# An attention and expert kernel: the order of TensorE's first instructions in the expert stage

## The chip, the cores and the metric

The kernel runs on one core of a Trainium2 chip. The metric is the device time of one execution in microseconds (us), told as the median of several runs. The engines of the core are named PE (TensorE matmul), PEld (TensorE weight load), DVE (VectorE), ACT (ScalarE), POOL (GpSimd) and SP (SyncE, which only issues DMAs here).

## The reference

A layer norm, cross attention with 16 heads over 8 sequences of 512 tokens and width 512, and a residual. Then a second layer norm and a layer of 8 experts, two for each token:

```
logits = flat @ router_weight.T + router_bias          # flat: 4096 tokens x 512
scores = softmax(logits); topk_vals, topk_idx = top_k(scores, 2)
w      = zeros(T, E) with topk_vals at topk_idx
gu     = einsum('th,ehf->tef', flat, gate_up_proj) + gate_up_bias
gate   = minimum(gu[..., :512], 7);  up = clip(gu[..., 512:], -7, 7)
act    = (up + 1) * gate * sigmoid(1.702 * gate)
down   = einsum('tei,eih->teh', act, down_proj) + down_bias
out    = einsum('teh,te->th', down, w);  result = x + out
```

## The kernel before, in words

Three stages follow each other: `attention_stage` (to about 970 us of the span), `routing_stage` (to about 1020 us) and `expert_stage`. Only the last is touched.

The expert stage works on 39 tiles of 256 token places; a tile belongs to one expert. For tile i the steps are these. POOL gathers the rows of the tokens into `xg` (`fetch`, L1540) with two indirect DMAs. PE turns them (`turn_rows`, L1279: 8 transposes of 128x128 into two PSUM tiles `t_ps`, four a tile; each half raises the mark `turned`). ACT copies each half to `xgT_hi` (`row_hi`, L1336) and DVE writes the remainder `xgT_lo` (`row_lo`, L1406), since each f32 product is made of three passes over high and low parts. PE makes gate and up in four quarters f (`gate_up`, L1295: 2 x 4 x 3 = 24 matmuls a quarter, 96 a tile) into four PSUM tiles `gu_ps`. DVE and ACT turn each quarter into a part of `hid` (L1414, L1416, L1362, L1421, L1424, L1368, L1429). PE makes the down product (`down`, L1309: 24 matmuls of 512 columns into `d_ps[0]` and `d_ps[1]`), DVE adds it to the sums (`mix`, L1447 and L1450), and POOL scatters the sums.

The weights come raw by DMA; ACT makes their high part (`gu_hi` L1254 for gate and up, `d_hi` L1257 for down) and DVE the low part (`gu_lo` L1260, `d_lo` L1263). That is done where a tile's expert differs from the one that the same buffer held, and for tiles 0 and 1 always.

Each engine has its own order, written out by hand, and waits on semaphores. PE's order is in `on_pe`: `turn_rows(0)`, and then for i from -1: `turn_rows(i + 2)`, `gate_up(i + 1)`, `down(i)`. So it begins turn 0, turn 1, gate and up 0, turn 2, gate and up 1, down 0, turn 3, gate and up 2, down 1. The waits of these steps that matter here are:

- `turn_rows(i)`: the gather of tile i, and for each half `xgT_lo_made[i - 1, half]`, since `t_ps` is one buffer.
- `gate_up(i, f=0)`: all four `wg_lo` of the buffer, and `xgT_lo_made[i, 1]`; from tile 1 on each quarter also waits for `up_made` of four quarters before.
- `down(i)`: `wd_lo`, `hid_lo` of each quarter, and `y_added[i - 1, j]`, which says that DVE has read `d_ps[j]` of the tile before (L1447).

ACT begins with the four `gu_hi` of tile 0 and `row_hi(0)`, then `row_hi(1)`, which waits for both halves of `turned` of tile 1, and behind it in its order the four `d_hi` of tile 0, the four `gu_hi` of tile 1, and the sigmoids and high parts of tile 0. DVE begins with `gu_lo` of tile 0, `row_lo(0)` and `pick_weight(0)`; then two `gu_lo` of tile 1; then, for tile 0, the clip of quarter 0, the third `gu_lo` of tile 1, `row_lo(1)`, `pick_weight(1)`, quarter 1, the fourth `gu_lo` of tile 1, and so on to `hidden_lo(0, 3)`. `mix(i - 1)` stands in the second quarter of tile i + 1. POOL's `fetch(3)` waits for `turned` of tile 1 and for `pick_weight(1)`. SP's loads for tile 3 wait for the `gu_lo` of tile 1.

Of the kernel before, what the change touches and what calls it, by code (L numbers as in the profile page):

```python
# [1192 lines left out]
def expert_stage(nc, raw, s_raw, xln_dram, w_stored, out, w_gate_up, w_down, b_gate_up, b_down, tile_hot, tile_expert, tile_changed, token_of, ident, n_tiles):  # L1193
    E, D, F2 = w_gate_up.shape
    F = F2 // 2
    KD, KF = D // P, F // P
# [8 lines left out]
    with ExitStack() as ctx:  # L1205
# [63 lines left out]
        def on_pe(e):  # L1269
            def turn_rows(i):  # L1270
                s = i % 2
                for half in range(KD // 2):
                    e.wait_ge(gathered[s], turn(i) * 16 * SUB)
                    if i:
                        e.wait_ge(xgT_lo_made.sem, xgT_lo_made[i - 1, half])
                    for k in range(2):
                        for j in range(SUB):
                            c = 2 * half + k
                            ins = e.transpose(t_ps[half][:, k, j * P:(j + 1) * P], xg[s][:, j, c * P:(c + 1) * P], ident[:, :])  # L1279
                    ins.then_inc(turned.sem, 1)  # L1280

            def gate_up(i, parts):
                s = i % 2
                for f in parts:
                    if f == 0:
                        e.wait_ge(wg_lo_made[s], turn(i) * KD)
                        e.wait_ge(xgT_lo_made.sem, xgT_lo_made[i, KD // 2 - 1])
                    n = i * KF + f
                    if n >= GU_BANKS:
                        e.wait_ge(up_made.sem, up_made[of_f[n - GU_BANKS]])  # L1290
                    for part in range(2):
                        cols = slice(part * F + f * P, part * F + (f + 1) * P)
                        for k in range(KD):
                            for m, (pw, px) in enumerate(PASSES):
                                ins = e.matmul(gu_ps[n % GU_BANKS][:, part, :], wg[s][pw][:, k, cols], xgT[s][px][:, k, :],  # L1295
                                               start=(k == 0 and m == 0), stop=(k == KD - 1 and m == len(PASSES) - 1))
                    ins.then_inc(gu_made.sem, 1)

            def down(i):
                s = i % 2  # L1300
                e.wait_ge(wd_lo_made[s], turn(i) * KF)

                order = [(k, j) for k in range(KF) for j in range(SUB)] if i < n_tiles - 1 else [(k, j) for j in range(SUB) for k in range(KF)]
                for k, j in order:
                    e.wait_ge(hid_lo_made.sem, hid_lo_made[i, k])
                    if k == 0 and i:
                        e.wait_ge(y_added.sem, y_added[i - 1, j])
                    for m, (pw, px) in enumerate(PASSES):
                        ins = e.matmul(d_ps[j][:, :], hid[s][px][:, k, j * P:(j + 1) * P], wd[s][pw][:, k, :],  # L1309
                                       start=(k == 0 and m == 0), stop=(k == KF - 1 and m == len(PASSES) - 1))  # L1310
                    if k == KF - 1:
                        ins.then_inc(down_made.sem, 1)

            turn_rows(0)
            for i in range(-1, n_tiles):
                if i + 2 < n_tiles:
                    turn_rows(i + 2)
                if i == n_tiles - 2:

                    gate_up(i + 1, range(KF // 2))  # L1320
                    down(i)
                    gate_up(i + 1, range(KF // 2, KF))
                    continue
                if i + 1 < n_tiles:
                    gate_up(i + 1, range(KF))
                if i >= 0:
                    down(i)

        def on_act(e):
            def row_hi(i):  # L1330
# [272 lines left out]
        with nc.Block() as block:  # L1603
            block.gpsimd(on_pool)
            block.sync(on_sp)
            block.scalar(on_act)
            block.vector(on_dve)
            block.tensor(on_pe)
# [79 lines left out]
```

## Time and profile before

| | us |
|---|---|
| median of 3 runs (lowest, highest) | 1759.33 (1756.08, 1760.47) |
| the profiled execution's own time | 1756.44 |
| its span, first to last instruction | 1754.7 |
| PE busy | 1617.4 (92%) |
| PEld busy | 1189.2 (68%) |
| DVE busy | 1246.5 (71%) |
| POOL busy | 801.6 (46%) |
| ACT busy | 659.0 (38%) |

The span lies inside the profiled execution; 1.74 us of the execution are outside it. Times in the rows are counted from the start of the span. Matmuls overlap, so the distance between two starts is the cadence, and it is shorter than the duration of one. "Granted clock" is the share of 2.4 GHz that PE was given: 0.50 is 1.2 GHz and 1.00 is 2.4 GHz. An engine's idle time is put down to the instruction that ended it.

### The profile page before, as it was taken

The page shows a single profiled execution, that of the slowest core. Times are in us where ns is not written, and L with a number is a line of the kernel's source. Part 1 is how long each engine was busy: PE and PEld are TensorE (multiplying, and loading weights), DVE is VectorE, ACT ScalarE, POOL GpSimd, SP SyncE. Part 2 cuts the span into 40 slices and gives each one's busy share as a digit, 9 for nine tenths or more (in the row PEclk, how much of TensorE's full clock was granted, in tenths as well). Part 3 has the DMA queues.
Part 4 walks back from the last instruction along what each step waited for, and adds up shares of the span by engine and source line. Part 5 has one row for each costly group of instructions (what it writes and reads, how often), then busy time and mean ns, then how long its engine had stood idle before and what let it go on. Part 6 is the DMA issues. An engine that isn't in the chain of part 4 may idle for free. (4 is left out here: it accounts for less than half of the span.)

```text
span 1754.7 us, 30046 instructions
## 1 busy us (share of the span) xinstructions
PE 1617.4 (92%) x9637; PEld 1189.2 (68%) x9637; DVE 1246.5 (71%) x2223; ACT 659.0 (38%) x1265; POOL 801.6 (46%) x619
## 2 busy tenths in 40 slices
PE   5889999999999999999987269999999999999995
PEld 3545555555565655556533269999999998999994
DVE  4675777777777767776664867777878778777873
ACT  3354544545445354454441033223333233222320
POOL 3364656556565655556564022333343433434332
PEclk9999999999999999999998569999999999999998
DMA  6342343434334334333311421324443353324321
GB/s 215 81 122 66 104 111 83 130 89 110 108 92 113 103 93 120 96 100 95 89 52 60 159 74 62 98 86 159 162 153 115 94 206 112 105 79 148 113 79 66
DMA packets 98804, 188.69 MB, mean 108 GB/s; under 512 B 26320, under 2 KB 27344, under 8 KB 98640
## 3 DMA queue, kind: packets, MB, share of 16 engines
q1 hardware_dynamic: 79408, 123.99, 25.0%
q0 software_dynamic: 19232, 62.73, 11.2%
q8 instruction: 77, 1.26, 0.3%
q14 instruction: 87, 0.71, 0.1%
HBM read 204.19 MB, written 37.36 MB: 138 GB/s over the span
## 5 line engine op out<-in xcount | busy, mean ns | idle before, releaser
L677 DVE TENSOR_REDUCE negmax<-max_ps 128x2 f32<-128x1024 f32 x256 | 312.4, 1220 | 203.7 <-PE max_ps L446 203.4
L566 ACT ACTIVATE pt<-work 128x512 f32<-128x512 f32 x512 | 278.4, 594 | 242.2 <-PE work L458 228.8
L760 POOL TENSOR_TENSOR acc<-acc,pt 128x1024 f32<-128x1024 f32 x128 | 303.8, 2377 | 121.8 <-ACT pt L566 121.8
L1295 PE MATMUL gu_ps<-xgT_hi,wg_hi 128*128 128x256 f32 x1248 | 355.3, 285 | 0.0
L1295 PE MATMUL gu_ps<-xgT_hi,wg_lo 128*128 128x256 f32 x1248 | 352.0, 282 | 0.0
L1295 PE MATMUL gu_ps<-xgT_lo,wg_hi 128*128 128x256 f32 x1248 | 351.8, 282 | 0.0
L757 POOL TENSOR_TENSOR acc<-pt 128x1024 f32<-128x1024 f32 x64 | 152.9, 2391 | 248.9 <-PE work L478 181.1
L1295 PEld LDWEIGHTS gu_ps<-xgT_lo,wg_hi 128*128 128x128 f32 x1248 | 235.8, 189 | 0.1
L1295 PEld LDWEIGHTS gu_ps<-xgT_hi,wg_hi 128*128 128x128 f32 x1248 | 235.7, 189 | 0.1
L1295 PEld LDWEIGHTS gu_ps<-xgT_hi,wg_lo 128*128 128x128 f32 x1248 | 235.6, 189 | 0.0
L1556 POOL DMA_INDIRECT out<-acc,idx x78 | 77.5, 994 | 325.0 <-DVE acc L1450 319.0
L446 PE MATMUL max_ps<-ks,qs 96*128 96x512 f32 x512 | 201.6, 475 | 24.0 <-DVE negmax L677 12.6
L1362 ACT ACTIVATE sig<-gate 128x256 f32<-128x256 f32 x156 | 65.1, 418 | 336.9 <-DVE gate L1414 335.2
L458 PE MATMUL work<-qs,ks 98*128 98x512 f32 x512 | 166.8, 405 | 7.4 <-DMA qs<-m_lo 6.0
L446 PEld LDWEIGHTS max_ps<-ks,qs 96*128 96x128 f32 x512 | 88.9, 193 | 85.5 <-issue 52.2
L470 PE MATMUL o_ps<-pt,v 128*32 128x512 f32 x1024 | 137.2, 608 | 1.6 <-ACT pt L566 1.6
L1309 PE MATMUL d_ps<-wd_hi,hid_hi 128*128 128x512 f32 x312 | 125.2, 401 | 9.7 <-DVE acc L1447 8.3
L1551 POOL DMA_INDIRECT acc<-out,idx x78 | 80.7, 1035 | 103.7 <-DMA out<-acc,idx 91.3
L688 DVE RECIPROCAL inv<-inv 128x128 f32<-128x128 f32 x128 | 120.7, 943 | 7.9 <-ACT inv L572 7.9
L413 PE MATMUL work<-xT,wq 128*128 128x512 f32 x256 | 125.8, 615 | 0.0
L1309 PE MATMUL d_ps<-wd_lo,hid_hi 128*128 128x512 f32 x312 | 124.7, 400 | 0.0
L1309 PE MATMUL d_ps<-wd_hi,hid_lo 128*128 128x512 f32 x312 | 124.5, 399 | 0.0
(201 smaller groups left out, 2803.0 us busy)
## 6 DMA issues: line engine op xcount, KB each, us to landing
raw_g<-w_gate_up SPq DMA_DIRECT2D x39, 2048.0 KB
raw_d<-w_down SPq DMA_DIRECT2D x39, 1024.0 KB
ks<-k_hi SPq DMA_DIRECT2D x252, 64.0 KB, 2.0
qs<-q_hi SPq DMA_DIRECT2D x252, 64.0 KB, 2.0
bd<-b_down SPq DMA_DIRECT2D x39, 256.0 KB
x_in<-x SPq DMA_DIRECT2D x32, 256.0 KB, 3.1
ctxT_raw<-ctx_t SPq DMA_DIRECT2D x32, 256.0 KB, 3.9
x<-x SPq DMA_DIRECT2D x32, 256.0 KB, 3.0
```

Source lines behind the costliest of these rows:

```text
L413: ins = e.matmul(to[:, :], wq[:, k, cols], xT[:, k, :], start=(k == 0), stop=(k == C - 1))
L446: ins = e.matmul(max_ps[:, j, :], qs[i][0:3 * HD, h, t * P:(t + 1) * P], ks[i][0:3 * HD, h, :], start=True, stop=True)
L458: e.matmul(to[:, :], ks[i][0:3 * HD + 2, h, k * P:(k + 1) * P], qs[i][0:3 * HD + 2, h, :], start=True, stop=True).then_inc(exp_ready.sem, 1)
L470: ins = e.matmul(o_ps[u % 2][HD * h:HD * (h + 1), :], v[:, k, c * P + HD * h:c * P + HD * (h + 1)], pt[k % 2][:, h, :], start=(k == 0), st ...
L566: e.activation(pt[k % 2][:, h, :], in_work("exp", u, k, h)[:, :], ACT.Exp, scale=scale).then_inc(exped.sem, 1)
L677: e.tensor_reduce(negmax[:, u % 2, n:n + 2], max_ps[:, :, :], AX.X, ALU.max, negate=True).then_inc(maxed.sem, 1)
L688: e.reciprocal(inv[:, cols], inv[:, cols]).then_inc(inverted.sem, 1)
L757: e.tensor_tensor(acc[:, heads, :], pt[0][:, heads, :], pt[1][:, heads, :], ALU.add).then_inc(added.sem, 1)
L760: e.tensor_tensor(acc[:, heads, :], acc[:, heads, :], pt[k % 2][:, heads, :], ALU.add).then_inc(added.sem, 1)
L1295: ins = e.matmul(gu_ps[n % GU_BANKS][:, part, :], wg[s][pw][:, k, cols], xgT[s][px][:, k, :], start=(k == 0 and m == 0), stop=(k == KD - 1 ...
L1309: ins = e.matmul(d_ps[j][:, :], hid[s][px][:, k, j * P:(j + 1) * P], wd[s][pw][:, k, :], start=(k == 0 and m == 0), stop=(k == KF - 1 and ...
L1551: e.indirect_dma_start(out=acc[s][:, j, :], out_offset=None, in_=out_rows, in_offset=slot_rows(i, j)).then_inc(acc_in[s], 16)
```

## The change

The first iteration of the loop (i = -1) is written out ahead of it. In it, quarter 0 of tile 0's gate and up now stands ahead of `turn_rows(1)`, and the quarters 1 to 3 behind it. All other steps of PE keep their order, and no other engine's order is changed.

```
             turn_rows(0)
-            for i in range(-1, n_tiles):
+
+            gate_up(0, range(1))
+            turn_rows(1)
+            gate_up(0, range(1, KF))
+            for i in range(n_tiles):
                 if i + 2 < n_tiles:
                     turn_rows(i + 2)
                 if i == n_tiles - 2:
...
                 if i + 1 < n_tiles:
                     gate_up(i + 1, range(KF))
-                if i >= 0:
-                    down(i)
+                down(i)
```

## Rows read from the trace of the kernel before

**Rows 1.** Chain that ended last, start of the expert stage: start us, us, what.
```profile
1025.21 5.31 DMA xg<-xln_dram,idx
...
1030.56 1.97 PE t_ps L1279 x8
1032.53 12.81 PE gu_ps L1295 x96
1045.34 0.87 PE t_ps L1279 x8
1046.21 11.40 PE gu_ps L1295 x96
```

**Rows 2.** DVE's timeline: start, us, instruction, count, idle before and what ended it.
```profile
1028.36 0.69 DVE L1406 TENSOR_TENSOR xgT_lo<-t_ps,xgT_hi 128x512 fp32r<-128x512 f32 x1 [0.16 <-issue]
...
1036.33 2.36 DVE L1260 TENSOR_TENSOR wg_lo<-raw_g,wg_hi 128x1024 fp32r<-128x1024 f32 x2 [6.99 <-ACT wg_hi L1254]
...
1040.60 1.28 DVE L1406 TENSOR_TENSOR xgT_lo<-t_ps,xgT_hi 128x512 fp32r<-128x512 f32 x2
...
1043.66 1.22 DVE L1260 TENSOR_TENSOR wg_lo<-raw_g,wg_hi 128x1024 fp32r<-128x1024 f32 x1
...
1054.83 0.17 DVE L1500 TENSOR_SCALAR bu<-bg 128x4 f32<-128x4 f32 x1 [1.62 <-PE gu_ps L1295]
...
1075.03 0.74 DVE L1447 SCALAR_TENSOR_TENSOR acc<-d_ps,w_slot,acc 128x512 f32<-128x512 f32 x1
...
1092.32 0.74 DVE L1447 SCALAR_TENSOR_TENSOR acc<-d_ps,w_slot,acc 128x512 f32<-128x512 f32 x1
...
1469.47 0.74 DVE L1447 SCALAR_TENSOR_TENSOR acc<-d_ps,w_slot,acc 128x512 f32<-128x512 f32 x1
```

**Rows 3.** ACT's timeline between 1033 and 1040 us.
```profile
1033.06 2.18 ACT L1257 ACTIVATE wd_hi<-raw_d 128x512 fp32r<-128x512 f32 x4
1035.14 3.89 ACT L1254 ACTIVATE wg_hi<-raw_g 128x1024 fp32r<-128x1024 f32 x4
```

**Rows 4.** PE's timeline from tile 0's first quarter to tile 1's gate and up.
```profile
1032.18 0.56 PE L1295 MATMUL gu_ps<-xgT_hi,wg_hi 128*128 128x256 f32 x1
1032.54 0.41 PE L1295 MATMUL gu_ps<-xgT_lo,wg_hi 128*128 128x256 f32 x1
...
1035.10 0.39 PE L1295 MATMUL gu_ps<-xgT_lo,wg_hi 128*128 128x256 f32 x1
...
1045.96 0.37 PE L1295 MATMUL gu_ps<-xgT_hi,wg_hi 128*128 128x256 f32 x1
```

**Rows 5.** Stretches: length, busy PE, PEld, DVE, ACT, POOL, clock, DMA, GB/s.
```profile
1035.00:1035.30 0.30, 0.30 (x3) 0.30 (x3) 0.00 (x0) 0.30 (x2) 0.00 (x0) 0.50 0.00 0
1035.30:1036.00 0.70, 0.70 (x8) 0.70 (x7) 0.00 (x0) 0.70 (x1) 0.00 (x0) 0.97 0.00 0
```

**Rows 6.** PE's timeline at the second product of down 1 and of down 2.
```profile
1076.00 0.39 PE L1309 MATMUL d_ps<-wd_hi,hid_hi 128*128 128x512 f32 x1
...
1093.85 0.40 PE L1309 MATMUL d_ps<-wd_hi,hid_hi 128*128 128x512 f32 x1
```

**Rows 7.** PE's timeline, matmuls behind the three longest idle gaps late in the stage.
```profile
1470.36 0.47 PE L1309 MATMUL d_ps<-wd_hi,hid_hi 128*128 128x512 f32 x1 [1.71 <-DVE acc L1447]
...
1718.67 0.48 PE L1309 MATMUL d_ps<-wd_hi,hid_hi 128*128 128x512 f32 x1 [2.51 <-DVE acc L1447]
...
1733.98 0.47 PE L1309 MATMUL d_ps<-wd_hi,hid_hi 128*128 128x512 f32 x1 [3.03 <-DVE acc L1447]
```

**Rows 8.** Stretches of PE: length, PE busy, clock, DMA share, GB/s.
```profile
1472.00:1473.00 1.00, 1.00 (x4) 0.62 0.16 61
1475.00:1476.00 1.00, 1.00 (x5) 0.67 0.41 154
1720.00:1722.00 2.00, 1.88 (x8) 1.00 0.34 131
1735.00:1736.00 1.00, 0.96 (x3) 0.53 0.00 0
```

## The prediction

> **What bounds the kernel now.** I read the chain of waits first, from the start of the expert stage. Its last link that is no TensorE work is the gather of tile 1's rows, which ends at 1025.21 + 5.31 = 1030.52; from there the chain is PE alone: 8 transposes in 1.97 us, tile 0's gate and up in 12.81, 0.87 for tile 2's transposes, 11.40 for tile 1's gate and up [rows 1]. So PE stands idle for a gather although tile 0's operands are there: DVE's timeline shows its last `xgT_lo` ending at 1028.36 + 0.69 = 1029.05 [rows 2]. That is the 1.5 us the change reaches for. The stretches say that all this runs at 1.2 GHz (granted clock 0.50) until 1035.30 and at 2.4 GHz from then on [rows 5].
>
> Then I asked who else is close. DVE's timeline from 1036.33 on shows it starting when ACT hands it tile 1's first `wg_hi` (6.99 us of idle, ended by L1254), and finishing the fourth `wg_lo` of tile 1 at 1043.66 + 1.22 = 1044.88 [rows 2]. PE starts tile 1's gate and up, which needs it, at 1045.96 [rows 4]: a slack of 1.08 us. ACT in turn began its `d_hi` and `gu_hi` at 1033.06 and 1035.14, as soon as it had copied tile 1's transposes [rows 3]. So besides PE's own order there is a second chain, tile 1's transposes, ACT, DVE, tile 1's gate and up, and it is only 1.08 us shorter.
>
> **PE's own gain.** All that PE issues from the first transpose of tile 1 to the end of tile 0's gate and up is the same 8 transposes and 96 matmuls. It now starts at 1029.05 plus a handoff instead of at 1030.56. A handoff from DVE to PE takes 1470.36 - (1469.47 + 0.74) = 0.15 us [rows 2, 7]; I use 0.13, a little less because both ends are rounded, so PE starts near 1029.2. By itself this is 1.4 us less.
>
> **What is moved later.** The transposes of tile 1 now come behind 24 matmuls. How long these take depends on the clock. At 1.2 GHz the distance of two starts is (1035.10 - 1032.54) / 12 = 0.213 us [rows 4]; at 2.4 GHz it is 11.40 / 96 = 0.119 us [rows 1]. In the trace the clock rose 4.74 us after the first of the transposes (1030.56) and 3.12 us after the first gate and up matmul (1032.18), at 1035.30. Three cases:
>
> - It rises 3.12 us after the new first matmul, at 1032.3: 15 slow ones, and 9 x 0.119 = 1.1 us, so the transposes start at 1033.4. They run fast.
> - It rises 4.74 us after it, at 1033.9: some 22 slow and 2 fast, transposes at 1034.2, fast.
> - It rises later than the transposes: 24 x 0.213 = 5.1 us and the first matmul's longer step (0.36 against 0.21), transposes at 1034.4, slow.
>
> From the start of the slow transposes to ACT's first `d_hi` the trace has 1033.06 - 1030.56 = 2.50 us [rows 1, 3]. Fast transposes take 1.97 - 0.87 = 1.10 less, which leaves 1.40. ACT's `d_hi` then begins at 1034.8, 1035.6 or 1036.9 instead of 1033.06: a delay d of 1.7, 2.5 or 3.9 us. I take the middle, 2.5, and keep both ends.
>
> **What hangs on it.** ACT's 4 `d_hi` and 4 `gu_hi` stand back to back behind `row_hi(1)` (2.18 and 3.89 us, rows 3), so tile 1's `wg_hi` is late by d, and so is DVE, which was waiting for it. From 1036.33 DVE has no wait that could take the delay in: the fourth `wg_lo` of tile 1 ends at 1044.88 + d = 1047.4, and tile 1's gate and up starts 0.13 later, at 1047.5 instead of 1045.96. That is d - 0.95 = 1.55 us later than before, although PE itself was ready 1.4 us sooner. The gain is gone, and PE waits some 2.5 us in front of that step, behind tile 2's transposes, which themselves wait for `row_lo(1)` (it began at 1040.60, now at 1043.1).
>
> DVE's lag is not used up there. The `bu` line of tile 1 (1054.83) stands behind an idle time of 1.62 us, between the last `hid_lo` of tile 0 and the first clip of tile 1, where DVE reads the flags of the next tiles and branches; tile 1's first quarter had been ready for it since 1046.2 + 24 x 0.119 = 1049.1 [rows 1, 2]. So I count it as DVE's own time and not as waiting. DVE is therefore behind PE for all of tiles 0 to 2, and carries the whole d up to `mix(0)`. Its second L1447 ends at 1075.03 + 0.74 = 1075.77; PE starts the product that needs it at 1076.00 [rows 2, 6]. With the handoff, that product starts at 1075.77 + 0.13 + d = 1078.4 instead of 1076.00: d - 0.10 = 2.4 us later. The PE line is only d - 0.95 late on arrival, so this second wait adds 0.85 us.
>
> One tile later the same pair is 1092.32 + 0.74 = 1093.06 and 1093.85 [rows 2, 6], 0.66 us of room after the handoff, and PE is now late by nearly as much as DVE: nothing is added. The other products of DVE aren't reached: tile 0's last `hid_lo` had ended by 1054.83 - 1.62 = 1053.21 and is needed by down 0 at 1046.21 + 11.40 = 1057.61; 1053.21 + 2.5 is still before that. POOL's gather for tile 3 waits for the moved transposes and for `pick_weight(1)` and is late by d too; it is needed only behind down 0, over 10 us later. SP's load for tile 3 waits for the same `wg_lo`; no copy of weights is on PE's chain there. Quarter 0 of tile 0 is ready sooner, but DVE reads it only behind `gu_lo` of tile 1, so nobody uses that.
>
> Behind tile 3 PE's steps and its waits hang on each other as before, the waits at expert changes too [rows 7], so a shift of the chain there is a shift of the end.
>
> **Sum.** -1.4 (PE's earlier start) + 2.95 (its wait for `wg_lo`) + 0.85 (its wait at down 1) = +2.4 us. On the profiled execution's own 1756.44 that gives 1758.8. That execution is at the low end of those shown; the three runs and it have a mean of 1758.1, and 2.4 on that is 1760.5, which is what I predict.
>
> **The clock in the new gap.** After tile 0's last quarter (near 1043.6) PE has only 0.87 us of transposes until 1047.5. Late in the stage gaps of 1.71, 2.51 and 3.03 us stand in front of down products [rows 7]. Behind the first the granted clock fell to 0.62 and came back near 1475.6 (0.67 over 1475 to 1476), behind the second it stayed 1.00, behind the third it fell to 0.53 [rows 8]. So such a gap may cost the clock or not. Where it does, 1472.2 to 1475.6 are 3.4 us at half rate: 16 matmuls of gate and up instead of 28, 1.5 us of PE's time.
>
> The Trainium skill ("TensorE: Matmul & The Clock Gate", the closing table "Why this matters for your kernels") says that an idle gap between bursts of matmuls of about the size of this one puts the engine back to the low clock. By that rule the fall would be the likelier case here, and the time that of the first rival. The rows side with it in two gaps of three.
> The same page (Part 1, "What's actually happening") says that the moment of the change doesn't follow the kernel's start and moves from run to run; by that rule d is spread over its three cases from one execution to the next, which this single trace can't show.
>
> **The rivals.**
>
> - *The clock falls in the new gap.* PE is then late by d - 0.95 + 1.5 = 3.05 at down 1, more than DVE's 2.4, so DVE adds nothing: +3.05, 1761.2. For it: two of the three gaps, and a gap longer than these. Against: the third, and the transposes within it. 0.3.
> - *DVE catches up before `mix(0)`.* If the 1.62 us ahead of the `bu` line are waiting and not its own, only the first wait is left: d - 0.95 = +1.55, 1759.7. Against it: tile 1's quarter was long ready. 0.1.
> - *All slow:* the clock rises behind the transposes, d = 3.9: +3.8, 1761.9, and up to +5 with a fall in the gap. 0.1.
> - *The other side: a late gather.* In the trace tile 1's rows land at 1030.52. Where they land later, the old order is late one for one, the new one not before its transposes' turn at 1034.2. At 1030.52 + 2.4 = 1032.9 both are even; at 1034.2 the old order has lost 3.7 and the new one 2.4: -1.3, 1756.8, and it doesn't get better than that. For it: the gather has been seen once, and took 5.31 us. Against: it would have to be 2.4 us later in most executions. 0.05.
>
> **How the numbers follow.** Forecast 0.45, the rivals as given. A measurement of this kernel tells about 0.3%, 5.3 us; its three runs lie 4.4 us apart. No case reaches 5.3 by itself, so what is outside is a case of +3 to +5 together with the spread of the medians: slower 0.07, faster 0.02, same 0.91. For the range, from 1756.8 (late gather) to 1763 (all slow, with a fall), and 1 to 2 us on the upper side for the spread of the runs: 1757 to 1765.
>
> **What would show it.** In the changed profile: 24 L1295 matmuls from near 1029.2; `xgT_hi` of tile 1 at 1034 to 1035 and `wd_hi` d later; PE idle for 2 to 3 us in front of tile 1's gate and up, put down to DVE L1260; a short PE wait for L1447 in down 1; the same distances as before from down 2 on. I am wrong in the mechanism if tile 1's gate and up starts before 1046, and in the size if d is not between 1.7 and 3.9 or if the chain behind tile 3 is late by something other than d - 0.1.

## The result and the profile after

The changed kernel takes 1762.73 us (median of 20 runs, 1760.16 to 1768.28), the kernel before 1758.89 (20 runs, 1755.18 to 1763.28). The ratio is 1.0025, 95% interval 1.0016 to 1.0033, so the change makes the kernel slower by 2.8 to 5.8 us. Ratios are of fast runs alone, here and below; of all the runs only one of e9b and one of the kernel before beside it were slow and are left out. I had forecast +2.4 and put it at 1760.5, within 1757 to 1765. The sign and the range held; the size is nearer to 4 us than to 2.4. Of the 2.2 us between 1760.5 and 1762.73, 0.8 is the kernel before, whose median of 20 runs lies above the 1758.1 that I had started from, and 1.4 is the change.

The profiled execution of the changed kernel took 1764.88 us, its span is 1763.2. Of the 8.5 us by which that span is longer, 3.6 lie ahead of the expert stage, where nothing was changed (ACT's first `wg_hi` starts at 1023.02 instead of 1019.42). I therefore count from that instruction, "the start of the stage", wherever two kernels are compared below. Line numbers behind the change are 3 higher than before.

The chain that ended last, in the changed kernel from the start of the stage on (start us, us, what). It is to be read against [rows 1]:

```profile
1023.02 1.07 ACT wg_hi L1254
1024.11 4.69 DVE wg_lo L1260 x4
...
1032.90 0.70 DVE xgT_lo L1409
1033.60 0.14 issue
1033.73 5.07 PE gu_ps L1295 x24
1038.80 0.45 PE t_ps L1279 x4
1039.27 0.60 ACT xgT_hi L1339
...
1041.81 0.63 ACT wd_hi L1257
1042.44 3.80 ACT wg_hi L1254 x4
...
1050.85 1.23 DVE wg_lo L1260
1052.08 0.04 issue
1052.13 13.04 PE gu_ps L1295 x96
1065.16 5.58 PE d_ps L1309 x24
```

Before, this stretch was the gather and then PE alone. Now the chain leaves PE behind quarter 0 and goes over ACT and DVE for 13 us, until tile 1's gate and up starts at 1052.13. That is 29.11 us from the start of the stage and was 1045.96 - 1019.42 = 26.54 [rows 4]: 2.57 later. Tile 1's gate and up then takes 13.04 us from its first start to its last end; counted in the same way it took 11.65 before (the 11.40 of [rows 1] leaves out the 0.25 us that overlap with the transposes ahead of it), so 1.39 more.

Tile 1's weights and DVE's steps in the changed kernel (start, us, instruction, count, idle before), against [rows 2, 3]:

```profile
1040.24 2.19 ACT L1257 ACTIVATE wd_hi<-raw_d 128x512 fp32r<-128x512 f32 x4
```
```profile
1043.52 2.36 DVE L1260 TENSOR_TENSOR wg_lo<-raw_g,wg_hi 128x1024 fp32r<-128x1024 f32 x2 [9.65 <-ACT wg_hi L1254]
...
1050.85 1.22 DVE L1260 TENSOR_TENSOR wg_lo<-raw_g,wg_hi 128x1024 fp32r<-128x1024 f32 x1
...
1082.22 0.75 DVE L1450 SCALAR_TENSOR_TENSOR acc<-d_ps,w_slot,acc 128x512 f32<-128x512 f32 x1
```

`wd_hi` starts 17.22 us into the stage instead of 13.64, so the delay I called d is 3.58 us. DVE's first `wg_lo`, its fourth and its second read of `d_ps` are late by 3.59, 3.59 and 3.59 us as well: once late, DVE takes nothing in up to `mix(0)`.

PE from its first matmul of gate and up over its waits, and at the product in down 1 that was to wait a second time:

```profile
1033.73 0.55 PE L1295 MATMUL gu_ps<-xgT_hi,wg_hi 128*128 128x256 f32 x1 [1.50 <-DVE xgT_lo L1409]
...
1038.14 0.30 PE L1295 MATMUL gu_ps<-xgT_hi,wg_lo 128*128 128x256 f32 x1
...
1048.62 1.23 PE L1279 MATMUL t_ps<-ident,xg 128*128 128x128 f32 x8 [0.41 <-DVE xgT_lo L1409]
1052.13 0.58 PE L1295 MATMUL gu_ps<-xgT_hi,wg_hi 128*128 128x256 f32 x1 [2.28 <-DVE wg_lo L1260]
...
1083.54 0.39 PE L1309 MATMUL d_ps<-wd_hi,hid_hi 128*128 128x512 f32 x1
```

The 1.50 us in the first row are PE's wait for tile 0's `xgT_lo`, which every order of PE has. The last row is 60.52 us into the stage, and was 56.58 [rows 6]: 3.94 later, without a wait. And the stretches around the wait for `wg_lo` (length, busy PE, PEld, DVE, ACT, POOL, granted clock, DMA share, GB/s):

```profile
1048.60:1049.90 1.30, 1.23 (x8) 0.83 (x8) 1.27 (x5) 0.12 (x1) 0.18 (x1) 1.00 0.00 0
1049.90:1052.10 2.20, 0.00 (x0) 0.00 (x0) 2.17 (x5) 0.72 (x2) 1.84 (x2) 0.94 0.24 45
1052.10:1055.10 3.00, 2.97 (x14) 2.98 (x15) 2.86 (x7) 0.84 (x2) 0.79 (x1) 0.50 0.48 151
1055.10:1056.10 1.00, 1.00 (x9) 1.00 (x9) 0.88 (x3) 0.00 (x0) 0.00 (x0) 0.93 0.03 4
```

The clock fell some 0.3 us before the end of the gap and stayed at 1.2 GHz for the first 3 us of tile 1's gate and up. This is the first rival of the prediction, with a larger d; the case that I had forecast, with the clock kept and a second wait in down 1, is not what happened.

### The profile page after: what moved, and what is told of

It is laid out like the page before. It is cut to its first block and busy times, and to the rows that moved or that the text cites. A ratio compares the mean times of both kernels' runs of the same rounds, so it can differ in the third digit from the quotient of the medians.

```text
span 1763.2 us, 30046 instructions
## 1 busy us (share of the span) xinstructions
PE 1621.0 (92%) x9637; PEld 1190.7 (68%) x9637; DVE 1247.0 (71%) x2223; ACT 659.0 (37%) x1265; POOL 802.4 (46%) x619
## 5 line engine op out<-in xcount | busy, mean ns | idle before, releaser
L1554 POOL DMA_INDIRECT acc<-out,idx x78 | 81.1, 1040 | 101.5 <-DMA out<-acc,idx 89.2
L458 PEld LDWEIGHTS work<-qs,ks 98*128 98x128 f32 x512 | 96.3, 191 | 41.3 <-issue 12.9
```

Of the source, the lines that this page charges most:

```text
L458: e.matmul(to[:, :], ks[i][0:3 * HD + 2, h, k * P:(k + 1) * P], qs[i][0:3 * HD + 2, h, :], start=True, stop=True).then_inc(exp_ready.sem, 1)
L1554: e.indirect_dma_start(out=acc[s][:, j, :], out_offset=None, in_=out_rows, in_offset=slot_rows(i, j)).then_inc(acc_in[s], 16)
```

## The experiments

The times of all experiments are medians of 6 to 12 runs (one run for e6), and the ratios, with their 95% intervals, are to the kernel before on the same chips. They are worked out from all these runs and so can differ by up to a tenth of a per cent from the ratio of two medians. This table collects what their profiles show, in us from the start of the stage: the first matmul of tile 0's gate and up, ACT's first `wd_hi`, the start of tile 1's gate and up, the start of down 1 and of down 2.

| kernel | gate/up 0 | wd_hi | gate/up 1 | down 1 | down 2 | ratio (95%) |
|---|---|---|---|---|---|---|
| before, 1st | 12.76 | 13.64 | 26.54 | 55.88 | 73.73 | |
| before, 2nd (e5) | 12.42 | 13.30 | 25.90 | 55.23 | 73.38 | 1.0010 (0.9998 to 1.0023) |
| before, 3rd (e6) | 12.94 | 13.82 | 26.43 | 55.89 | 73.91 | |
| changed, 1st | 10.71 | 17.22 | 29.11 | 59.83 | 77.68 | 1.0025 (1.0016 to 1.0033) |
| changed, 2nd (e1) | 10.78 | 17.56 | 29.43 | 60.31 | 78.15 | 1.0029 (1.0016 to 1.0041) |
| half a quarter ahead (e3) | 10.10 | 15.24 | 27.10 | 56.64 | 75.33 | 1.0005 (0.9994 to 1.0017) |
| two quarters (e9b) | 10.45 | 20.29 | 32.17 | 63.40 | 81.24 | 1.0038 (1.0025 to 1.0051) |
| four quarters (e2) | 11.05 | 25.83 | 37.70 | 69.04 | 86.89 | 1.0067 (1.0047 to 1.0088) |
| changed, gap filled (e4) | 10.10 | 16.88 | 28.76 | 58.30 | 76.96 | 1.0023 (1.0008 to 1.0039) |
| changed, ACT reordered (e7) | 10.92 | 17.58 | 26.19 | 55.52 | 73.37 | 0.9995 (0.9984 to 1.0006) |
| before, ACT reordered (e8) | 12.43 | 14.64 | 25.74 | 55.07 | 72.92 | 0.9990 (0.9981 to 1.0000) |

**The changed kernel again (e1).** No edit.

> The changed kernel once more, for a second profile of it. Its first profile showed ACT's d_hi late by d = 3.6 us against the kernel before (counted from the start of the stage), tile 1's gate and up late by d - 1.0, the clock at half rate for the first 13 matmuls behind the wait, and down 1 late by 3.9 us. Chain theory (transposes, ACT, DVE, tile 1's gate and up): d between 1.7 and 3.9 again, and down 1 late by the larger of d - 0.1 (clock kept) and d - 1.0 + 1.5 (clock fallen); +2 to +4.5 us in the time. Rival, run noise: the 3.6 us by which the routing stage already began later in the first profile belongs to the change and comes back here. The chain theory expects it to be anything between -3 and +4, since nothing ahead of the expert stage is changed.

1764.01 us. The stage began at 1021.31 here; in the ten profiles in this table other than this one it began between 1018.33 and 1023.02, with the old order at 1019.42, 1021.78 and 1021.47. So the 3.6 us ahead of the stage in the first profile belong to the spread of the executions and not to the change. Inside the stage the picture came back, with d = 3.92 against the first profile of before:

```profile
1050.74 0.58 PE L1295 MATMUL gu_ps<-xgT_hi,wg_hi 128*128 128x256 f32 x1 [2.28 <-DVE wg_lo L1260]
```

**More and fewer quarters ahead (e2, e3, e9b).** If the moved transposes hold up ACT and DVE, the cost follows the number of matmuls put ahead of them; if the cost is the clock alone, it doesn't.

```
# e2
-            gate_up(0, range(1))
+            gate_up(0, range(KF))
             turn_rows(1)
-            gate_up(0, range(1, KF))
```
```
# e3: gate_up is told which halves (gate, up) of a quarter to make
-            def gate_up(i, parts):
+            def gate_up(i, parts, halves=range(2)):
...
-            gate_up(0, range(1))
+            gate_up(0, range(1), range(1))
             turn_rows(1)
+            gate_up(0, range(1), range(1, 2))
             gate_up(0, range(1, KF))
```
```
# e9b
-            gate_up(0, range(1))
+            gate_up(0, range(2))
             turn_rows(1)
-            gate_up(0, range(1, KF))
+            gate_up(0, range(2, KF))
```

In e3 the waits stand ahead of the first half and the mark that the quarter is made behind the second.

> All four quarters of tile 0's gate and up stand ahead of turn_rows(1). Chain theory: the transposes start behind 96 matmuls instead of 24, near 13 us after PE's start, so d is 10 to 11 us, PE idles some 8 to 10 us in front of tile 1's gate and up, ended by wg_lo, the clock falls, and the end is late by 9.5 to 12 us against the kernel before. Rival, PE's order alone (the transposes are cheap wherever they stand, and the change's cost is the clock): no more than the change itself, +2 to +4. Rival, DVE has slack that takes the delay in before mix(0): about +9 less what it takes in, 5 to 7.

> Only half of quarter 0 (its gate part, 12 matmuls) stands ahead of turn_rows(1), the up part behind it. Chain theory: transposes start 2.7 us after PE's start instead of 5.3, d = 1.0 to 2.0, tile 1's gate and up late by d - 1.0 = 0 to 1, the gap in front of it under 1.5 us so that the clock stays, down 1 late by d - 0.1: +1 to +2 us in the time, about half of the change. Rival, the clock fall is all that costs: 0 or below (-1.4), since no gap is long enough. Rival, any split costs the same: +3.8 as the change.

> Two quarters of tile 0's gate and up ahead of turn_rows(1). Counted from the start of the stage (ACT's first wg_hi); the kernel before has ACT's first wd_hi at 13.3 to 13.8 in three profiles, tile 1's gate and up at 25.9 to 26.5 and down 2 at 73.4 to 73.9. Chain theory, now with its own numbers: first matmul at 10.1 to 11.0, transposes 8.2 us behind it (about 22 slow and 26 fast), wd_hi 1.6 behind these, at 19.9 to 20.9; wg_lo of tile 1 complete 11.8 later and its gate and up 0.13 behind that, at 31.8 to 32.8, after 5 us or so of idle; the clock falls (+1.4); down 2 at 80 to 81.5, so 6.5 to 7.7 us late; time +6.5 to +7.7. It lies between one quarter (+4) and four (+13). Rival, the loss is that of the clock and doesn't grow with the number of quarters: +4. Rival, two quarters give DVE work early and the lag shrinks: +5.

1769.58, 1759.83 and 1764.91 us. Against the mean of the three profiles of before (`wd_hi` at 13.59, down 2 at 73.67) the four kernels with 12, 24, 48 and 96 matmuls ahead have d of 1.65, 3.6 to 4.0, 6.70 and 12.24 us, and down 2 late by 1.66, 4.0 to 4.5, 7.57 and 13.22. The expectations for one half, two and four quarters put the end at +1 to +2, +6.5 to +7.7 and +9.5 to +12. At down 2 the first two held, and the third was low by 1 us, since I had expected d at 10 to 11. In the times, two and four quarters are clearly slower, by 6.5 and 10.2 us in the medians; the half quarter, whose interval runs from 0.9994 to 1.0017, isn't told from the kernel before. All of d is carried on; what comes on top with two and four quarters, 0.9 and 1.0 us, is the fall of the clock behind the waits, less the room of some 1 us that PE had in front of the second chain. It is more than in the changed kernel, since tile 1's gate and up took 13.55 and 13.66 us there and not 13.04. The waits of PE in the kernels with four and with two quarters ahead:

```profile
1056.92 1.94 PE L1279 MATMUL t_ps<-ident,xg 128*128 128x128 f32 x8 [8.93 <-DVE xgT_lo L1408]
1060.43 0.58 PE L1295 MATMUL gu_ps<-xgT_hi,wg_hi 128*128 128x256 f32 x1 [1.56 <-DVE wg_lo L1260]
```
```profile
1046.99 1.37 PE L1279 MATMUL t_ps<-ident,xg 128*128 128x128 f32 x8 [3.25 <-DVE xgT_lo L1409]
1050.50 0.58 PE L1295 MATMUL gu_ps<-xgT_hi,wg_hi 128*128 128x256 f32 x1 [2.13 <-DVE wg_lo L1260]
```

With only half a quarter ahead the gap was 1.28 us and the clock stayed. There the second wait of the prediction is seen, in down 1 (its second product), and down 2 is late by d:

```profile
1047.87 0.39 PE L1295 MATMUL gu_ps<-xgT_hi,wg_hi 128*128 128x256 f32 x1 [1.28 <-DVE wg_lo L1260]
...
1078.86 0.47 PE L1310 MATMUL d_ps<-wd_hi,hid_hi 128*128 128x512 f32 x1 [0.51 <-DVE acc L1452]
```
```profile
1046.00:1048.00 2.00, 0.72 (x7) 1.00 0.33 64
1048.00:1050.00 2.00, 2.00 (x17) 1.00 0.52 135
```

(The second fence has length, PE busy, granted clock, DMA share and GB/s.)

**The gap filled (e4).** The products of the filler are thrown away.

```
                     turn_rows(i + 2)
+                if i == 0:
+                    for _ in range(18):
+                        e.matmul(d_ps[0][:, 0:FTOK], xgT[1][0][:, 0, 0:P],
+                                 xgT[1][0][:, 0, :], start=True, stop=True)
```

> The changed kernel with 18 extra matmuls of 256 columns on tile 1's turned rows into d_ps[0] (which down 0 overwrites) between tile 2's transposes and tile 1's gate and up: 2.1 us of work in a gap of some 2.3 us, so that the clock has no idle stretch to fall in. The extra products are thrown away. Chain theory with the clock as a separate term: granted clock 1.00 through the gap, tile 1's gate and up takes 11.4 us and not 13.0, and the end is late by d - 0.1 (2.0 to 3.5 us) and not by d + 0.5: 0.6 us less than e1 at the same d. Rival, the fall costs the full 1.5 us of the time: 1.5 us less than e1. Rival, the filler itself delays PE: as e1 or more.

1762.51 us. PE's timeline and the stretches in it (length, PE busy, granted clock, DMA share, GB/s):

```profile
1045.56 1.23 PE L1279 MATMUL t_ps<-ident,xg 128*128 128x128 f32 x8 [0.40 <-DVE xgT_lo L1412]
1046.55 2.39 PE L1324 MATMUL d_ps<-xgT_hi 128*128 128x256 f32 x18
1049.07 0.39 PE L1295 MATMUL gu_ps<-xgT_hi,wg_hi 128*128 128x256 f32 x1
...
1080.06 0.47 PE L1309 MATMUL d_ps<-wd_hi,hid_hi 128*128 128x512 f32 x1 [0.51 <-DVE acc L1453]
```
```profile
1046.00:1048.00 2.00, 2.00 (x18) 1.00 0.03 8
1048.00:1049.00 1.00, 0.94 (x8) 1.00 0.44 58
1049.00:1051.00 2.00, 1.93 (x16) 1.00 0.58 141
```

The clock stayed at 2.4 GHz and the first wait was as long as before, only filled. PE came to down 1 at 58.30, 1.5 to 2.0 us sooner than in the two profiles with the fall, and then waited there for DVE; down 2 began at 76.96, which is 3.29 us late at d = 3.29. So the fall of the clock is real (tile 1's gate and up takes 1.4 to 1.5 us longer with it), but in this profile keeping it away gives back only what lies above d. From the table that is 77.68 - 76.96 - (17.22 - 16.88) = 0.38 us and, for e1, 0.51. That is read from one profile of this kernel. The times don't settle it: the medians of e4 and e1 are 1.50 us apart, as the rival with the full price says, but their ratios, 1.0023 and 1.0029, have intervals of 1.2 to 1.6 thousandths to either side, over 2 us, so 0.4 and 1.5 us both fit. What speaks against the rival is PE's wait of 0.51 us in the row above.

**The kernel before again (e5, e6).** No edit.

> The kernel before, for a second profile. The first one had tile 0's rows landing 6.3 us and tile 1's 11.1 us after the start of the stage (ACT's first wg_hi); four of the five profiles of changed kernels had tile 0's at 6.6 to 7.6. Theory, the first profile was an early one: tile 0's transposes start 6.6 to 7.6 us in, tile 1's perhaps later too, by up to 1 us, and down 1 starts at 55.9 to 56.9 (55.9 in the first); the cost of the change is then d less that, 3 to 4 us. Rival, the gather of tile 1 often lands 2.4 us later or more: down 1 at 58 or later. No change in the time.

> The kernel before, for a third profile; as for the second. With the two others it gives the spread of the landing of tile 1's rows and of down 1, 55.9 to 56.9 us from the start of the stage.

1759.32 and 1760.28 us. PE's first two waits in the stage, second and third profile of before:

```profile
1029.01 1.97 PE L1279 MATMUL t_ps<-ident,xg 128*128 128x128 f32 x8 [9.41 <-DMA xg<-xln_dram,idx]
1032.58 1.97 PE L1279 MATMUL t_ps<-ident,xg 128*128 128x128 f32 x8 [1.60 <-DMA xg<-xln_dram,idx]
```
```profile
1028.59 1.97 PE L1279 MATMUL t_ps<-ident,xg 128*128 128x128 f32 x8 [9.31 <-DMA xg<-xln_dram,idx]
1032.79 1.97 PE L1279 MATMUL t_ps<-ident,xg 128*128 128x128 f32 x8 [2.23 <-DMA xg<-xln_dram,idx]
```

Tile 0's transposes start 7.23 and 7.12 us into the stage and not at 6.31 as in the profile of the prediction, tile 1's at 10.80 and 11.32 (11.14 there). The idle stretch in front of tile 1's transposes, which the change wants to use, is 1.60 and 2.23 us and not 2.87. Of it 1.50 us are the wait for tile 0's `xgT_lo`, which the new order has too, so what was there to be gained is 0.10 and 0.73 us, and 1.37 in the profile of the prediction. In the seven profiles of kernels with matmuls ahead of the transposes, the first of these started at 10.10 to 11.05. So the idea saves about 0 to 1 us on PE and not 1.4. The rival with the late gather fell: in the three profiles tile 1's transposes start within 0.6 us of each other.

The two profiles also show that the second chain was closer than the one profile of the prediction had it. There DVE's second read of `d_ps` left 0.10 us of room behind the handoff. Here the product in down 1 that needs it is already held up (DVE's read and PE's product in e5):

```profile
1077.04 0.74 DVE L1447 SCALAR_TENSOR_TENSOR acc<-d_ps,w_slot,acc 128x512 f32<-128x512 f32 x1
```
```profile
1077.92 0.47 PE L1309 MATMUL d_ps<-wd_hi,hid_hi 128*128 128x512 f32 x1
```

Down 1 takes 6.04 and 5.92 us from first start to last end in these two, and 5.75 in the first profile. So in two executions of three DVE already cost PE 0.2 to 0.3 us before anything was changed, and each further delay of DVE goes into down 2 whole.

**ACT's order (e7, e8).** This takes away what made the delay expensive: ACT makes tile 1's `wg_hi` before it waits for tile 1's transposes. e7 has the changed order of PE, e8 the old one.

```
             row_hi(0)
+            changed = changed_flag(e, 1)
+            for k in range(KD):
+                gate_up_hi(1, k, changed)
             for i in range(-1, n_tiles - 1):
...
                         d_hi(e, 0, k)
-                    changed = changed_flag(e, 1)
-                    for k in range(KD // 2):
-                        gate_up_hi(1, k, changed)
-                if i + 2 < n_tiles:
+                if i >= 0 and i + 2 < n_tiles:
```

> The changed order of PE, and ACT makes tile 1's four wg_hi right behind row_hi(0), ahead of row_hi(1) and of tile 0's wd_hi, instead of behind them. Nothing that the moved transposes hold up then feeds tile 1's wg_lo before quarter 1. Chain theory: wg_hi of tile 1 at 9 to 10 us from the start of the stage, no PE wait for wg_lo, no fall of the clock, tile 1's gate and up at 25 to 26 us (26.5 before), and the time -1.5 to 0 against the kernel before: the change's loss of 3.8 us is gone altogether. Rival, the loss is in the order of PE itself or in the clock: still +3 to +4 us. Rival, another wait takes over (xgT_lo of tile 1, behind the clip of quarter 0 on DVE, or DVE's mix(0)): +1 to +2.

> The old order of PE with ACT's tile 1 wg_hi first, as in the run before this. Chain theory: PE had 1.1 us of room in front of tile 1's gate and up and waited for nothing, so DVE's earlier wg_lo buys nothing: tile 1's gate and up at 26.5 us, down 1 at 55.9, the time -0.5 to +0.5. Against it the new order with the same ACT should be 0.5 to 1.4 us better. Rival, DVE's lag was costing something later: -1 to -2.

1757.71 and 1758.37 us. ACT's timeline in e7:

```profile
1032.88 3.90 ACT L1254 ACTIVATE wg_hi<-raw_g 128x1024 fp32r<-128x1024 f32 x4 [0.26 <-issue]
1039.18 1.09 ACT L1339 ACTIVATE xgT_hi<-t_ps 128x512 fp32r<-128x512 f32 x2 [2.40 <-PE t_ps L1279]
1040.15 2.19 ACT L1257 ACTIVATE wd_hi<-raw_d 128x512 fp32r<-128x512 f32 x4
```

and the chain that ended last in it:

```profile
1033.49 5.21 PE gu_ps L1295 x24
1038.71 0.87 PE t_ps L1279 x8
1039.58 8.54 PE gu_ps L1295 x72
1048.13 0.87 PE t_ps L1279 x8
1049.00 11.40 PE gu_ps L1295 x96
```

`wd_hi` is as late as in the changed kernel (17.58), but PE doesn't wait, the chain stays on it, and the clock holds. Down 2 is at 73.37, where the kernel before has 73.38 to 73.91. The whole loss of the change is gone by moving one block on another engine, with PE's order as in the change. The interval, 0.9984 to 1.0006, lies wholly below that of the changed kernel. That the new order would then be 0.5 to 1.4 us better than the old one didn't show: e8 is 0.45 us ahead at down 2, and in the times the medians put e7 first and the ratios e8, so they can't be told apart. Neither e7 nor e8 is told from the kernel before by its time; e8's interval, 0.9981 to 1.0000, only just reaches 1. For e8 I had expected nothing to be gained, with down 1 at 55.9. It is at 55.07, and down 2 at 72.92 is 0.46 us ahead of the soonest of the three profiles of before: 0.16 us were there at down 1 and the rest is the wait for DVE in down 1, which e8 doesn't have.

## Why the prediction was right, and where it was off

- *The idle time for tile 1's rows.* There, but oversized. I took PE's first matmul at 1029.2, 9.8 us into the stage; it came at 10.7. My trace had tile 0's rows landing 0.8 to 0.9 us sooner than two further profiles of the same kernel. The term -1.4 is right for the trace that I read (1.37 us), and would have been -0.10 and -0.73 in the two others.
- *The clock's rise and d.* I took some 22 matmuls at 1.2 GHz and transposes at high clock. The changed kernel has the clock rising 4.4 us behind the first matmul (the row at 1038.14 is the first short one) and 20 matmuls at 1.2 GHz; its second profile has 5.0 us and some 22. The transposes start 4.9 and 5.2 us behind the first matmul, near the 5.0 that I had worked out. Of my cases the middle one was near. It took the distance of the rise from PE's first work behind its idle time, 4.74 us; this distance is 3.96 to 4.77 us in the four profiles with PE's old order (from tile 1's transposes) and 3.83 to 5.50 us in the seven with matmuls ahead (from the first of these). The first case took it from the first matmul of gate and up, 3.12 us, which is 2.34 to 3.15 us in the old order and in no profile of the new one. The case with transposes at 1.2 GHz came in e3 alone, where they take 1.91 us. The transposes' start to `wd_hi` is the last step: I took 1.40 us for it; it is 1.60. So of the 1.1 us by which d = 2.5 was too small, 0.9 is the later start of the stage's matmuls and 0.2 this step. This is the term that was mis-sized, and its cause is one gather read from one execution.
- *The wait for `wg_lo`.* d - 0.95 was worked out; it is 2.57 at d = 3.58. Right, and right too at d = 1.60, 6.65 and 12.19 but for 0.1 us: 0.56, 5.63 and 11.16.
- *DVE carries d whole.* Right in all profiles in which ACT's order is the old one. The 1.62 us ahead of `bu` stayed (1.61 in the changed kernel) although DVE was 3.6 us later: it is DVE's own time, and the rival that DVE catches up fell.
- *The second wait, in down 1.* Right where the clock stays (e3, e4: 0.51 us each); I had d - 0.10 and found down 2 late by d, since the 0.10 us of room is there in only one of the three profiles of before. In the changed kernel the wait doesn't occur, since the fall of the clock makes PE later than DVE there, by 0.4 us.
- *The clock in the gap.* I gave its fall 0.3 as a rival; it happened in both profiles of the changed kernel and in those with two and four quarters, and not behind the gap of 1.28 us. The rule of the Trainium skill that I cited ("TensorE: Matmul & The Clock Gate", "Why this matters for your kernels") pointed this way, and the trace agrees in the direction: idle for 2.28 us behind transposes of 1.23 us, granted clock 0.50 from 1052.1 on. How long a gap has to be for it the runs don't settle, since in the kernel before the clock fell behind 1.71 us and not behind 2.51 [rows 7, 8], each with another 0.5 us of waiting three matmuls later. The rival's price was right (1.5 taken; tile 1's gate and up takes 1.4 and 1.5 us longer in the two profiles), and its sum d - 0.95 + 1.5 gives 4.1 us at the true d, for 3.95 seen. The forecast should have been this case.
- *The rest of the kernel.* The time from down 2 to the last DMA issue is 655.4 to 657.6 us in three profiles of before and 656.7 and 656.9 in two of the changed kernel. A shift at down 2 is a shift of the end, with a spread of some 2 us that is there without the change. Over all eleven profiles it is 653.8 (e3) to 657.6 us, so the end alone can't show a shift of 1 or 2 us.
- *The signs I had named.* Tile 1's gate and up does not start before 1046, so the mechanism stands. By my own sign the size does not: the chain is late from down 2 on by d + 0.4 and not by d - 0.1.

Together: -1.4 should have been some -0.4 and d 3.6, the fall of the clock takes the place of the second wait, and the chain is 4.0 to 4.5 us late at down 2 against the mean of three profiles; the medians of the times say 3.8 and 4.7. The sign was forecast from the right chain. That the size came within the range owes to a range drawn wide enough for the rivals, and not to the case that I had put first.

## What to carry to other kernels

A step on the bounding engine that fills its idle time also moves whatever stands behind it. Before doing so, follow what waits for that, through the other engines' hand-written orders, to where it comes back; here a chain over ACT and DVE was only 1.08 us shorter than PE's own, so 5 us of matmuls ahead of 1 us of transposes cost more than the 0.1 to 1.4 us of idle time could give. The delay was fixed on the engine that carried it (work that needs nothing new put ahead of the wait), not on the one that was changed; that took away the loss and made no gain that the times could show. And a gain of 1.5 us read from one gather in one execution is within what that gather moves by itself: look at several.

## What the runs showed of the hardware

- The same two indirect DMAs of 128 rows for tile 0 let PE start its transposes between 6.31 and 7.58 us into the stage in eleven profiles, with nothing changed ahead of them; POOL issued the four gathers of the two tiles at the same times of the stage to within 0.02 us in all eleven, so the spread lies between its instructions and the landing. Tile 1's transposes start at 10.80 to 11.32 us in the four with PE's old order.
- The granted clock rose 14.77 to 15.95 us into the stage in the eleven profiles, and 3.83 to 5.50 us behind the work with which PE ended its last idle time before it (tile 1's transposes or tile 0's gate and up).
- Filling a 2.3 us gap with 18 matmuls whose products nobody uses kept the granted clock at 1.00 (one profile), where the same gap left idle gave 0.50 for the 3 us behind it (two profiles).
- The fall cost 1.4 to 1.5 us of matmul time and 0.4 to 0.5 us of the chain, because DVE was due just behind it. Behind two idle stretches (8.93 and 1.56 us in e2, 3.25 and 2.13 us in e9b) tile 1's gate and up took 2.0 and 1.9 us longer, not 1.4.
